# Running expert counts on VectorE and a two-product prefix in the merged mixer and router of a macaron layer

## The reference, cut to what matters

```python
logits = x2d @ router_w.T + router_b          # 16 experts
vals, idx = jax.lax.top_k(logits, 2)
flat_e = idx.reshape(-1)
oh = (flat_e[:, None] == jnp.arange(E)[None, :]).astype(jnp.int32)
pos = jnp.take_along_axis(jnp.cumsum(oh, axis=0) - 1, flat_e[:, None], axis=1)[:, 0]
kept = pos < capacity                         # capacity 1280
slot = flat_e * capacity + pos
...
x = x + 0.5 * ffn(layernorm(x))
x = x + mixer(layernorm(x))
x = x + 0.5 * ffn(layernorm(x))
```

## Time and profile before

| | |
|---|---|
| median of 3 runs | 3237.86 us (3231.03 to 3239.02) |
| the profiled execution | 3226.07 us |
| its span, first to last instruction | 3224.4 us |
| VectorE busy over the span | 62% |
| TensorE matmul busy over the span | 87% |
| mean granted TensorE clock | 0.960 of full speed |
| one-hot counts of the sixteen groups in the merged stage | from 1456.9 to 2237.7 us |

### The profile page before, as it was taken

How to read it: one execution, slowest core, us unless ns; L and a number is a source line. 1 busy time by engine, 2 the same in 40 slices (tenths; PEclk the granted TensorE clock), 3 DMA queues, 4 the chain that set the end, 5 groups by cost and what they waited for, 6 DMA issues and landing times. The chain is left out here.

```text
span 3224.4 us, 63582 instructions
## 1 busy us (share of the span) xinstructions
PE 2817.3 (87%) x22016; PEld 2270.6 (70%) x22016; DVE 1993.7 (62%) x4585; ACT 1574.5 (49%) x2719; POOL 1267.1 (39%) x1072
## 2 busy tenths in 40 slices
PE   4452999999999995899989999985799999999997
PEld 4452888888888883466756666664688888888886
DVE  4443566566665653578888888853565666656664
ACT  3441555565565652344434343421455655656553
POOL 2543222232322323456676767744122323223233
PEclk9999999999999997899999999965899999999999
DMA  9824444454454426501111111101554544544444
GB/s 306 286 83 105 81 87 86 83 86 77 86 92 84 82 38 159 173 15 41 33 45 36 39 41 41 35 29 47 116 91 84 85 75 86 92 85 81 78 73 145
DMA packets 569797, 281.28 MB, mean 87 GB/s; under 512 B 397879, under 2 KB 552571, under 8 KB 569440
## 3 DMA queue, kind: packets, MB, share of 16 engines
q1 hardware_dynamic: 511680, 203.20, 25.9%
q0 software_dynamic: 57888, 75.16, 13.5%
HBM read 142.44 MB, written 146.41 MB: 90 GB/s over the span
## 5 line engine op out<-in xcount | busy, mean ns | idle before, releaser
L727 POOL DMA_INDIRECT acc_a<-ae_ob,ae_to x160 | 260.8, 1630 | 698.5 <-ACT ae_ob L680 644.4
L727 POOL DMA_INDIRECT acc_b<-be_ob,be_to x150 | 244.9, 1632 | 657.8 <-ACT be_ob L680 605.8
L698 ACT ACTIVATE be_h<-be_pH,b 128x512 f32<-128x512 f32 (+1 forms) x384 | 236.7, 616 | 374.9 <-PE be_pH L625 349.3
L698 ACT ACTIVATE ae_h<-ae_pH,b 128x512 f32<-128x512 f32 (+1 forms) x384 | 236.6, 616 | 364.0 <-PE ae_pH L625 346.9
L1469 POOL TENSOR_TENSOR m_xf<-m_tmp,m_xT 128x512 f32<-128x512 f32 x160 | 181.2, 1159 | 120.2 <-DVE m_tmp L1190 120.1
L434 POOL DMA_INDIRECT slots_a<-ar_row,ar_sidx x128 | 125.7, 982 | 152.4 <-issue 143.9
L1522 POOL DMA_INDIRECT slots_b<-m_row,m_sidx x128 | 152.6, 1192 | 83.9 <-issue 83.9
L1764 PEld LDWEIGHTS m_PP<-m_RP,m_KS 64*64 64x64 f32 x6656 | 122.5, 140 | 87.6 <-issue 86.5
L1764 PE MATMUL m_PP<-m_RP,m_KS 64*64 64x64 f32 x6656 | 137.3, 227 | 36.9 <-DVE m_A L1220 35.9
L1233 DVE TENSOR_TENSOR m_RP<-m_RP,m_tot 128x512 f32<-128x512 f32 x96 | 92.0, 958 | 85.8 <-PE m_PP L1764 85.8
L1190 DVE SCALAR_TENSOR_TENSOR m_tmp<-m_B,m_ch,m_xx 128x512 f32<-128x512 f32 x160 | 112.0, 741 | 45.7 <-PE m_B L1854 38.1
(11 more groups left out here) (340 smaller groups left out, 9110.8 us busy)
## 6 DMA issues: line engine op xcount, KB each, us to landing
ae_stage<-in_w SPq DMA_DIRECT2D x64, 512.0 KB
be_stage<-in_w SPq DMA_DIRECT2D x64, 512.0 KB
slots_a<-empty SPq DMA_DIRECT2D x10, 2080.0 KB, 19.2
slots_b<-empty SPq DMA_DIRECT2D x10, 2080.0 KB, 19.0
ae_xq<-slots_a SPq DMA_DIRECT2D x256, 64.0 KB
be_xq<-slots_b SPq DMA_DIRECT2D x256, 64.0 KB
ar_xin<-in_x SPq DMA_DIRECT2D x16, 512.0 KB
acc_a<-ar_xin SPq DMA_DIRECT2D x16, 512.0 KB
```

The costliest lines, as they stand in the source:

```text
L698: t = act.activation(dst[:, 0:SIZES[b]], pH[c % 2][:, 0:SIZES[b]], ACT.Gelu, bias=S.b1[:, bass.ds(i * (2 * FC) + (u * FC + f), 1)])
L727: pool.indirect_dma_start(S.acc[tag][:, :], bass.IndirectOffsetOnAxis(ap=to[m][:, q:q + 1], axis=0), ob[m][:, q, :], None, bounds_check=T ...
```

## The change

The diff touches `mix_and_route` alone. The tiles sumc and seen go. A tile run[u] of 128 x 4 x 16 holds, for each tile of a group, the count of all tiles before it, earlier groups included. VectorE adds run[u][j+1] = run[u][j] + cnt[u][j] three times in a chain, then signals run_ready; a fourth add puts the first entry of the next group's run[1-u], after the wait that the prefix of group g - 1 is done, and VectorE waits for it. The prefix is two products: `before` times cnt, and all ones times run[u], each over 64 columns. TensorE waits for run_ready in place of counts_ready and seen_ready.

```diff
-        sumc = sb("sumc", [P, E])
-        seen = [sb(f"seen{u}", [P, E]) for u in range(2)]
+        run = [sb(f"run{u}", [P, GQ, E]) for u in range(2)]
...
                     dve.tensor_tensor(cnt[u][:, :, :], ohk[:, :, 0, :], ohk[:, :, 1, :],
                                       ALU.add).then_inc(counts_ready, 1)
+                    dve.wait_ge(counts_ready, g + 1)
+                    for j in range(GQ - 1):
+                        ins = dve.tensor_tensor(run[u][:, j + 1, :], run[u][:, j, :], cnt[u][:, j, :], ALU.add)
+                        if j < GQ - 2:
+                            c(ins)
+                            c.settle()
+                    ins.then_inc(run_ready, 1)
                     if g + 1 < NG:
-                        dve.wait_ge(counts_ready, g + 1)
-                        c(dve.tensor_reduce(sumc[:, :], cnt[u][:, :, :].rearrange("p q e -> p e q"), AX.X, ALU.add))
+                        dve.wait_ge(run_ready, g + 2)
+                        filled(dve, "C", g - 1)
+                        c(dve.tensor_tensor(run[1 - u][:, 0, :], run[u][:, GQ - 1, :], cnt[u][:, GQ - 1, :], ALU.add))
                         c.settle()
-                        filled(dve, "C", g - 1)
-                        dve.wait_ge(seen_ready, g + 1)
-                        dve.tensor_tensor(seen[1 - u][:, :], seen[u][:, :], sumc[:, :],
-                                          ALU.add).then_inc(seen_ready, 1)
...
-                dve.memset(seen[0][:, :], 0.0).then_inc(seen_ready, 1)
+                dve.memset(run[0][:, 0, :], 0.0).then_inc(run_ready, 1)
+                dve.wait_ge(run_ready, 1)
...
                 def prefix(g):
                     u = g % 2
-                    pe.wait_ge(counts_ready, g + 1)
-                    pe.wait_ge(seen_ready, g + 1)
+                    pe.wait_ge(run_ready, g + 2)
                     b = fill("C", g)[:, 0:GQ * E].rearrange("p (q e) -> p q e", e=E)
                     pe.matmul(b, S.before[:, :], cnt[u][:, :, :], start=True, stop=False)
-                    for j in range(GQ - 1):
-                        pe.matmul(b[:, j + 1:, :], S.ones[:, :],
-                                  cnt[u][:, j:j + 1, :].to_broadcast([P, GQ - 1 - j, E]), start=False, stop=False)
-                    fills_up(pe.matmul(b, S.ones[:, :], seen[u][:, :].unsqueeze(1).to_broadcast([P, GQ, E]),
-                                       start=False, stop=True), "C", g)
+                    fills_up(pe.matmul(b, S.ones[:, :], run[u][:, :, :], start=False, stop=True), "C", g)
```

More of the change, by code:

```diff
@@ L1005, in mix_and_route @@
         free = [sem(f"free{k}") for k in range(NBK)]
-        rshift_ready, rown_ready, row_ready, dif_ready, ex_ready, counts_ready, seen_ready = (
+        rshift_ready, rown_ready, row_ready, dif_ready, ex_ready, counts_ready, run_ready = (
             sem(n) for n in ("rshift_ready", "rown_ready", "row_ready", "dif_ready", "ex_ready", "counts_ready",
-                             "seen_ready"))
+                             "run_ready"))
         mv_ready, rmv_ready, var_ready, rvar_ready, root_part = (
```

## The result

The change makes the kernel **slower by 1.0%**: 3268.26 us (3261.72 to 3273.01, six runs) against 3235.60 us (3231.03 to 3239.02, six runs) of the kernel before on the same chip, ratio 1.0100 [1.0084, 1.0116]. The forecast was 3245.9 us with a range to 3255.0; it fell short by 22 us. The profiled execution took 3262.32 us, its span 3260.6 us.

A forecast was written before the change was run, and what follows sets the result against it. VectorE's work in `choose` was taken as the path, with TensorE following. 15 x 0.42 = 6.3 us for the adds, less 0.63 for group 15, plus 2.3 for the clock gave +8.0 us: 3245.9 us, range 3238 to 3255.

The forecast's parts named there:

- the path: VectorE in `choose`, count to factors 5: the adds cost 0.42 us more per group, and the delay reaches the next group whole.
- the collision rival: VectorE's adds collide with GpSimd's power, the first starting 0.68 us late: +16 us, 3254 us; chance 0.04.
- the products: TensorE's prefix: three removed products, 0.64 us per group, are worth nothing, since VectorE's copy releases level 7.
- group 15: Last group, where VectorE waits for the prefix at half clock: 0.63 us less, once.
- the clock term: TensorE's falls to half clock: two at 1.10 us and six at 0.29, against 1.7 us now: +2.3 us.
- the clock falls behind the prefix in most groups: Rival, between `low` and level 7: ten falls at 1.10 us each, +15 us in all, 3253 us; chance 0.22.
- that the step holds nothing else that depends on phase: Everything but the adds, group 15 and the clock priced at nothing; no DMA and no SP or GpSimd queue changes.

The follow-up runs named there:

- e4: Kernel before with its reduction and its add to seen moved behind `places`, five products kept; ratio 0.9960 to the kernel before.
- e7: The kernel before, unchanged, run again; ratio 1.0005 to the kernel before.
- e3: Kernel after with its adds in two levels instead of a chain and the add for the next group moved behind `places`; ratio 0.9993 to the kernel before.
- e8: Kernel after with only the fourth add and its wait moved behind `places`, the chain of three kept; ratio 1.0012 to the kernel before.
- e5: The kernel after, unchanged, run again on the other kind of chip; ratio 1.0042 to the kernel before.
- the first pair: The first measurement of the kernels before and after on one chip: 3235.60 and 3268.26 us, ratio 1.0100.
- e1: Kernel before, five products kept, with two dummy adds chained behind the add to seen, about 0.41 us more of VectorE per group; ratio 1.0038.
- e2: Kernel after with three products of a zero tile with the ones matrix put back between the prefix's two; ratio 1.0050 to the kernel before.
- e10: The kernel after, unchanged, run again on the kind of chip with late releases; ratio 1.0105 to the kernel before.
- e9: Kernel after with idle zero-tile products, two ahead of the wait for running counts and three between the prefix's two; ratio 1.0060 to the kernel before.
- e11: Kernel after with GpSimd's second scatter call put ahead of its power instead of behind it; ratio 1.0065 to the kernel before.
- e12: Repeat of the kernel before with its reduction and its add to seen moved behind `places`; ratio 0.9968 to the kernel before.
- e17: Another unchanged repeat of the kernel before with its reduction and its add to seen moved behind `places`; ratio 0.9970 to the kernel before.

## Why the prediction was wrong, point by point

**Right: the path.** VectorE's time from count to factors 5 is the path, and reaches the next group whole. Undisturbed distances are 54.07 us with -0.53, 54.60 with nothing, 54.67 with +0.07, about 54.73 with +0.12, and 55.01 to 55.05 with +0.42 (e4, e7, e3, e8, e5 and the first pair). Each microsecond put on or taken off counts as one. One exception has no cause in the record: in group 6 of every kernel after, on both kinds of chip, factors 5 start at 1.32 us, 0.26 us idle behind the fourth add. The adds are 174 ns each and 0.205 us apart, inside GpSimd's power too, so the collision rival is out. The rule of the Trainium skill named for it (SBUF — State Buffer, Who interferes with whom) agrees at line 1511 before and does not at the power.

The other rule of the Trainium skill weighed there (VectorE: DVE Perf Modes, The DRAIN you can't avoid: between eight copies a semaphore costs nothing extra) does not hold for these short instructions: 0.09 against 0.20 us in e3, and the measurement decides.

**Right: the products.** Between two and five there is no difference on B (e1 beside e5, e2 beside e5, e3 beside e7). On A no run has five products with the delay.

**Right: group 15.** The last rows of the stage, TensorE then VectorE, beside the earlier trace rows:

```profile
2272.07 0.69 PE L1945 MATMUL m_B<-m_cnt,before 128*128 128x64 f32 x2 [3.18 <-DVE m_run L1325]
2272.55 0.63 PE L1946 MATMUL m_B<-m_run,ones 128*128 128x64 f32 x2
```

```profile
2271.16 0.23 DVE L1321 TENSOR_TENSOR m_cnt<-m_oh 128x64 f32<-128x64 f32 x1
...
2273.22 0.29 DVE L1341 TENSOR_TENSOR m_pex<-m_oh,m_B 128x128 f32<-128x128 f32 x1 [1.21 <-issue]
```

The prefix is done 2.02 us behind the count (2.05 forecast); `places` starts at 2.06 where it was 2.71, 0.65 us less against the forecast 0.63.

**Wrong: the clock term.** "I take two at 1.10 and six at 0.29 ... +2.3 us". It took the loss for small since most groups of the kernel before show no fall, and it used the price of a fall there. On B the term measures 4.7 us over eleven distances, on A, by subtraction, 7.0 (e10) to 10.8 over thirteen. The count was off: three falls behind the prefix on B, in eleven groups, where the kernel before has one, and seven or eight in thirteen on A. So was the price: a group with such a fall takes 1.35 to 2.0 us more (2.8 in group 1 on A, where it lasts 6.83 us), not 1.10, because the fall now lies on the transposes and a second one later in the group is longer. The rival "the clock falls behind the prefix in most groups" names the event that happened in eight of thirteen groups on A; it too used 1.10 us, left out the late releases, and so ended at 3253. The forecast gave it 0.22.

**Wrong: that the step holds nothing else that depends on phase.** The prediction says "No DMA and no queue of SP or GpSimd changes", and prices everything but the adds, group 15 and the clock at nothing. GpSimd's instructions are indeed the same, but not their timing: the long pattern of scatters in all thirteen groups before became the short one in ten. And on A, nine completions of level 7 come up to 2.7 us late in the kernel after and none in the kernel before. No row of before shows such a release, and the range had no room for it: 11.7 us. With 10.8 in place of 2.3 for the clock the forecast would have been 3254.4, still inside its range; this step put the result outside. With both it would have been 3266.

**Open.** What holds TensorE's signals. It is seen on A alone, in the kernel after (twice) and in e9. There every late group has the short pattern of scatters and no group with the long one is late, but group 13 in both traces of the kernel after and group 11 in e10 are short and on time, and on B all short ones are. That the scatters have a part in it is argued and not shown, as is that the delay alone would bring it. The kernels that could tell (e1, e11 and their repeats) all landed on B, where e1 and e5 agree and neither has one.

The version with the carry off the path (e4, e12, e17) is the one to keep: 0.3 to 0.4% under the kernel before, 9.6 to 12.6 us. Of these the distances between the first and the last count show 5.0 us in e4 (773.80 against 778.81 in e7) and 10.4 in e17 (768.43). It was not run on A.

## What to carry to other kernels

In a pipeline bound by dependences, price each edit by the instructions that it puts between two links of the path, not by what it saves on a busy engine: three products less on an engine at 87% were worth nothing here, four short adds on the path cost 0.4% on one kind of chip and 1.0% with what they set off on the other. Look first for what can leave the path: the running sum was needed a whole group later, and moving it beat both ways of computing it. And when a delay widens an idle time of TensorE, count the falls of the clock again and price each by the instructions on which it will now lie. Last, look what another engine starts within a few hundredths of a microsecond of the new place: here it was factors 5 and a scatter.

## What the runs showed of the hardware that was not expected

- TensorE's signals can be held together: level 7's event comes 1.8 to 2.7 us behind the start of the last product (0.23 us otherwise), for VectorE and ScalarE at the same moment, and the next signals follow 0.09 us apart. On A this happens in nine groups of the kernel after (first pair and e10) and in twelve of e9 (1.0 us in one); on three chips of kind B in none.
- The same edit costs 1.0100 and 1.0105 on one kind of chip and 1.0042 and 1.0045 on the other; a ratio from one chip is not the ratio.
- Idle products on a zero tile around the prefix, some 2.5 us of TensorE per group, made the kernel after faster by 14.6 us (3258.56 to 3243.94), with the clock at 1.00 in group 4.
- Two engines that meet within 0.05 us can come out either way from group to group: a scatter of 1.58 us in place of 1.06, or factors 5 of 0.77 us in place of 0.69. Beside `totals` factors 5 took 1.52 us (e11).
